# A graph kernel: TensorE reads an edge group's places four values at a time instead of up to 24

## The reference, cut to what matters

```python
edge_index = jnp.stack([src, dst])
h = jnp.maximum(_layernorm(x, axis=-1), 0.0)
W = jnp.zeros((1024, 1024)).at[row, col].add(edge_weight)   # row, col = src, dst
x = x + h @ W.T + L0_gnn_bias
h = jnp.maximum(_layernorm(x, axis=-1), 0.0)
# two layers, each: agg = segment_sum(h[src], dst); mean = agg / max(deg, 1)
#                   h = h @ W_self + mean @ W_neigh + b     (relu after the first)
return x + h
```

## Time and profile before

| | |
|---|---|
| median of 3 runs | 784.9 us (784.1 to 787.94) |
| the profiled execution | 788.07 us |
| its span, from the first to the last instruction | 786.3 us |
| PE busy | 748.0 us, 95% of the span |
| mean granted clock of TensorE | 0.987 of full |

### The profile page before, as it was taken

How to read it: one execution, slowest core, us unless ns; L and a number is a source line. 1 busy time by engine, 2 the same in 40 slices (tenths; PEclk the granted TensorE clock), 3 DMA queues, 4 the chain that set the end, 5 groups by cost and what they waited for, 6 DMA issues and landing times.

```text
span 786.3 us, 13475 instructions
## 1 busy us (share of the span) xinstructions
PE 748.0 (95%) x4433; PEld 619.4 (79%) x4434; DVE 584.0 (74%) x813; ACT 355.2 (45%) x596; POOL 478.5 (61%) x593
## 2 busy tenths in 40 slices
PE   2878999999999999899999999999999999999997
PEld 2767888888878788788888888888888888887886
DVE  7989378778545789985768775445698867589895
ACT  7757734333254357542325655543232223244731
POOL 5000057676748899775666382416799766755982
PEclk9689999999999999999999999999999999999999
DMA  3112455865566863465875625865843577776475
GB/s 113 43 53 90 139 156 191 257 204 187 185 214 202 280 220 97 149 212 182 301 234 178 190 91 149 291 207 200 293 162 108 194 235 261 257 249 209 155 238 193
DMA packets 82873, 148.78 MB, mean 189 GB/s; under 512 B 10795, under 2 KB 20898, under 8 KB 82800
## 3 DMA queue, kind: packets, MB, share of 16 engines
q1 hardware_dynamic: 62862, 105.07, 41.4%
q10 hardware_dynamic: 19938, 42.79, 15.3%
HBM read 106.42 MB, written 41.41 MB: 188 GB/s over the span
## 4 chain that ended last, share of the span: by engine, by line
PE 71%; DVE 13%; POOL 7%; issue 5%; DMA 2%; ACT 1%; SPq 0%; POOLq 0%; DVEq 0%; ACTq 0%
PE bank L1705 33%; PE bank L1755 20%; PE bank L1639 12%; DVE L L1938 3%; POOL split L1096 2%; DVE slot L2075 2%; DVE R L1923 2%; DVE L L1930 1%; DMA stage<-hT_scratch 1%; POOL T L1111 1%; POOL T L1113 1%; POOL S L1082 1%; PE bank L1535 1%; PE bank L1551 1%; PE bank L1771 1%
## 5 line engine op out<-in xcount | busy, mean ns | idle before, releaser
L1705 PE MATMUL bank<-slot,split 128*128 128x512 f32 x1680 | 386.4, 390 | 5.3 <-POOL split L1096 3.0
L1705 PEld LDWEIGHTS bank<-slot,split 128*128 128x128 f32 x1680 | 313.6, 188 | 72.1 <-issue 4.9
L1058 POOL TENSOR_TENSOR AT<-AT,az 128x50 int32 (+3 forms) x288 | 97.9, 340 | 120.8 <-DMA az<-asum_scratch 79.2
L1755 PE MATMUL bank<-slot,Ax 128*128 128x512 f32 x500 | 119.0, 392 | 0.2
L1096 POOL TENSOR_TENSOR split<-stage,split 128x512 fp32r<-128x512 f32 x50 | 67.3, 1348 | 76.8 <-ACT split L1324 76.7
L1755 PEld LDWEIGHTS bank<-slot,Ax 128*128 128x128 f32 x500 | 92.8, 188 | 20.3 <-issue 1.4
L2075 DVE TENSOR_TENSOR slot<-T,slot 128x512 fp32r<-128x512 f32 x64 | 91.8, 1466 | 9.7 <-ACT slot L1315 8.9
L1639 PE MATMUL bank<-slot,split_m 128*128 128x512 f32 x320 | 91.1, 396 | 0.0
L1324 ACT CAST split<-stage 128x512 fp32r<-128x512 f32 x50 | 31.1, 623 | 122.1 <-PE bank L1705 69.0
L1113 POOL TENSOR_TENSOR T<-T,wst 128x512 f32<-128x512 f32 x48 | 69.5, 1467 | 4.4 <-DMA wst<-in_L_gnn_W_self 4.4
L1639 PEld LDWEIGHTS bank<-slot,split_m 128*128 128x128 f32 x320 | 58.5, 188 | 11.1
(11 more groups left out here) (223 smaller groups left out, 1133.1 us busy)
## 6 DMA issues: line engine op xcount, KB each, us to landing
stage<-hT_scratch SPq DMA_DIRECT2D x90, 256.0 KB, 3.4
wst<-in_L_gnn_W_neigh SPq DMA_DIRECT2D x56, 256.0 KB, 4.6
wst<-in_L_gnn_W_self SPq DMA_DIRECT2D x56, 256.0 KB, 3.3
x1b_scratch<-x ACTq DMA_DIRECT2D x10, 512.0 KB, 5.3
hT_scratch<-hTs ACTq DMA_DIRECT2D x10, 512.0 KB, 3.3
wst<-prod0g_scratch SPq DMA_DIRECT2D x20, 256.0 KB, 3.5
hT_scratch<-h1s ACTq DMA_DIRECT2D x20, 256.0 KB, 3.4
wst<-prod1g_scratch SPq DMA_DIRECT2D x20, 256.0 KB, 3.7
```

The lines of the kernel that those rows point to most:

```text
L1058: pool.tensor_tensor(a, a, az32[:, n % NZ, pairs * pos:pairs * (pos + 1)], ALU.add) \
L1705: last = pe.matmul(dense_bank(v, which)[:, :], split[:, v % 2, a, NT * k:NT * (k + 1)], slot[t % 2][:, b, HF * (HK * which + k):HF * (HK * ...
L1755: last = pe.matmul(sums, Ax[:, u % NR_A, NT * k:NT * (k + 1)], part, start=(begins and k == 0 and b == 0), stop=(k == PAIRS - 1 and b == 1 ...
```

## The change

Places are no longer loaded ahead of three groups at once. Before each of the groups 3 to 36 there is a load of that group's own places: 4 values in groups 3 to 5, and from group 6 on the first four (chunks 0 to 3). The second four (chunks 4 to 7) are loaded in the middle of the group's products, before those of chunk 3. Bases are loaded only where they are used: one value ahead of group 3 (that of group 7), four in the middle of group 8 (of 10, 12, 14 and 16, every second entry of the table), then four at a time in the middle of groups 16, 20, 24, 28 and 32, before the products of chunk 4. TensorE has 68 loads of `tab_o` where it had 14, and 7 of `tab_w` where it had 4. No product, wait, DMA or instruction of another engine is added or removed.

```diff
-AT_ONCE = 24
-BASES = {3: range(4, 8), 8: range(8, 16), 15: range(16, 32), 31: range(32, LATE)}
+BASES = {3: range(7, 8), 8: range(10, 17, 2)}
+BASES.update((j, range(j + 1, j + 5)) for j in range(16, LATE - 1, 4))
@@
             def column_sums(j):
                 q, r = j % NQ, j % NR
                 for c in range(GC):
+                    if c == GC // 2 - 1 and SHARED[j] == 1:
+                        load_offsets(j, GC // 2, GC)
+                    if c == GC // 2 and j > 3 and j in BASES:
+                        load_bases(j)
@@
-            def load_offsets(j):
-
-                each = GC // SHARED[j]
-                upto = j + 1
-                while upto < LATE and SHARED[upto] == SHARED[j] and each * (upto + 1 - j) <= AT_ONCE:
-                    upto += 1
-                values = load(pe, tab_o[0:1, GC * j:GC * upto:SHARED[j]], 0, (WW - WD) * TW)
+            def load_offsets(j, first, last):
+
+                share = SHARED[j]
+                values = load(pe, tab_o[0:1, GC * j + first:GC * j + last:share], 0, (WW - WD) * TW)
+                offsets_of.update(((j, first // share + n), value) for n, value in enumerate(values))
+
+            def load_bases(j):
+
+                at = BASES[j]
+                base_of.update(zip(at, load(pe, tab_w[0:1, at.start:at.stop:at.step], 0, F)))
@@
-                if j not in offsets_of:
-                    load_offsets(j)
-                if j in BASES:
-                    if j == 3:
-                        pe.wait_ge(s_tabw, 16)
-                    base_of.update(zip(BASES[j], load(pe, tab_w[0:1, BASES[j].start:BASES[j].stop], 0, F)))
-                offsets = offsets_of[j]
+                load_offsets(j, 0, GC if SHARED[j] > 1 else GC // 2)
+                if j == 3:
+                    pe.wait_ge(s_tabw, 16)
+                    load_bases(j)
```

More of the change, by code:

```diff
@@ L1534, in column_sums @@
                     for part in range(3):
-                        last = pe.matmul(w_bank(j)[:, bass.ds(offsets[c // SHARED[j]], kw(j))], row,
+                        last = pe.matmul(w_bank(j)[:, bass.ds(offsets_of[(j, c // SHARED[j])], kw(j))], row,
                                          L[:, q, c, ka(j) + kw(j) * part:ka(j) + kw(j) * (part + 1)],
@@ L1567, in _ @@
             offsets_of, base_of = {}, {}
-            def load_offsets(j):
-                each = GC // SHARED[j]
-                upto = j + 1
-                while upto < LATE and SHARED[upto] == SHARED[j] and each * (upto + 1 - j) <= AT_ONCE:
-                    upto += 1
-                values = load(pe, tab_o[0:1, GC * j:GC * upto:SHARED[j]], 0, (WW - WD) * TW)
-                offsets_of.update((n, values[each * (n - j):each * (n - j + 1)]) for n in range(j, upto))
+            def load_offsets(j, first, last):
[5 more added lines that the diff above has]
+                base_of.update(zip(at, load(pe, tab_w[0:1, at.start:at.stop:at.step], 0, F)))
             for j in range(LATE):
```

## The result

The changed kernel took **790.69 us** (median of 4 runs, 789.9 to 791.57), the kernel before 784.55 in the same session (4 runs, 784.1 to 787.94). The ratio is **1.0059, 95% interval 1.0035 to 1.0082**: slower, by 4.6 us by the ratio and by 6.1 between the two medians. I had forecast 785.7, a range of 776 to 796, and "within 0.5%" as the likeliest. The profiled execution of the changed kernel had 791.57 us, span 789.8, mean granted clock 0.995.

What follows compares the result with a forecast made beforehand. TensorE was taken as the bound, its sequencer pacing the edge stage. Stretches of -1.1, +1.5, -1.7, +1.0, +0.8 and +0.3 summed to +0.8 us, taking the median from 784.9 to 785.7; range 776 to 796.

Steps and rivals of the forecast that it cites:

- the sequencer sets the pace: Edge stage: TensorE's sequencer, not the array (1.49 and 1.73 us a group), paces every group at 2.0 to 2.2; 62%.
- The pitch of groups without a base load: TensorE, edge stage: 1.27 + 0.39 + 0.47 = 2.13 us a group with a set end, 2.02 without.
- A hole of 0.3 before chunk 3: Sign in each group's products: about 0.3 us idle at the middle load, where the kernel before had none.
- Fours of places: TensorE's register loads of four neighbouring places: 0.37 us each, bounds 0.348 and 0.43.
- Rival B: Middle loads covered by queued products, so the array's 1.49 and 1.73 us pace groups: 773, half covered 779; 20%.
- rival C: A load amid running products costs 0.59 us, as loads of five or eight did: 14.7 us more, 800; 12%.
- rival D: Evenly spread holes keep the granted clock at half in groups 21 to 36: +13 us, 799; 6%.
- The length of a load by its fours: Register loads: values come in pieces of four, 0.10 us + 0.251 a piece; entries not neighbours one by one, 0.23 each.
- 12 to 20: Edge stage stretch: seven groups with set ends, two without, bases in 16 and 20: 19.9 against 21.62 us, -1.7.
- 27 to 35: Edge stage stretch: nine groups at 2.13 us and two base loads at 0.47: 20.1 against 19.29 us, +0.8.
- part two: Bases: five loads of four neighbours mid-group at 0.47 us each, one of every second entry in group 8 at 1.12.
- the reference: Starting point of the forecast: profiled execution of the kernel before, 788.07 us, 3.2 above the median of 784.9.

Runs made afterwards that it cites:

- experiment 4: Kernel before with at most 8 places in a load instead of 24, nothing else changed: 781.95 us, ratio 0.9939.
- 7: Kernel before with eight places read in one load ahead of each group, bases early and starting at multiples of four: 780.27 us, ratio 0.9929.
- 8: As 7, but from group 6 on places in two loads of four, the second ahead of chunk 3: 784.74 us, ratio 0.9979 to the kernel before.
- 9: As 7, but from group 6 on sixteen places (two groups) in one load: 783.2 us, ratio 0.9947 to the kernel before.
- experiment 1: Changed kernel with base ranges moved to start at multiples of four, eight middle loads where six stood: 787.88 us, ratio 1.0024 to the kernel before.
- experiment 3: Kernel before with only the bases loaded as in the changed kernel, places still 24 at once: 791.6 us, ratio 1.0081.
- 2: Kernel before with only the places loaded as in the changed kernel, bases as before: 785.63 us, ratio 1.0008.
- 5: Changed kernel with each middle load of places written twice; the pairs were merged, so the same kernel again: 790.99 us, ratio 1.0054 to the kernel before.
- 10: As 7, but bases 16 to 36 in one load in group 2, none later: 778.89 us, ratio 0.9895 to the kernel before.

## Why the prediction was right, and where it was not

The time lay inside the range, 5 us above the number; "within 0.5%", the likeliest outcome, did not come, and "slower", held at 0.30, did. The path was the one forecast, one term of its sum was too small by a factor of three, and the range was wide enough for that.

**What held.** That the sequencer sets the pace, and the model of its time. The pitch of groups without a base load, forecast at 2.13 with a set end and 2.02 without, was 2.14 in group 25; the five of groups 21 to 26 other than 24 average 2.07. A hole of 0.3 before chunk 3 was forecast, 0.29 came. Fours of places were forecast at 0.37 and took 0.33, strided ones at 1.02 and took 0.99. The same sums gave the pitch of experiment 4 (1.88, measured 1.90) and the difference of 7 and 8 (5, measured 4.61). Rival B (covered loads, 20%) fell by the changed kernel's own pitch and by 7 and 8; rival C (0.59 us for a short load amid products) by the 33 loads with a median of 0.332; rival D by the clock of 1.00 from group 21 on. The length of a load by its fours held too: 0.10 + 0.25 a piece makes 0.60 for eight neighbours and 1.10 for sixteen, and they took 0.59 (experiment 4) and 1.12 (9) in the median. That the entry at which a four begins counts as well, experiment 1 shows: 0.337 us in the median where the changed kernel's took 1.00 to 1.20.

**Stretch by stretch**, forecast against measured: to group 6 -1.1, measured -1.41; groups 6 to 11 +1.5, +1.27; 12 to 20 -1.7, -0.30; 21 to 26 +1.0, +1.18; 27 to 35 +0.8, +2.38; group 36 +0.3, +0.34. The two that miss most are those with two base loads each. Groups 21 to 26, with one, hide it, as their other loads came cheaper than 0.37.

**The step that failed** is part two, "five loads of four neighbours ... at 0.47 each". They took 1.20, 1.20, 1.00, 1.00 and 1.11 us: 5.53 where 5 x 0.37 = 1.85 was counted, 3.7 too little. Experiment 1 gives it back by moving the ranges (3.53 us at the last product, all but 0.35 of it by loads of this kind), and experiment 3 has it without the places' part. I had the piece of four from the rows of before, but every load there starts at a multiple of four, so these could not show what it hangs on; I took "neighbours" for the condition. The ranges 17 to 20, 21 to 24 stood in the diff. An operation whose start the trace never showed should have had 1.02, the price of the strided four, as its upper bound; then the case would have reached 5 x (1.02 - 0.37) = 3 us further up.

**The second miss** is the reference. The stage was late by 3.46 us, the medians differ by 6.1 and the ratio says 4.6. I carried the profiled execution's 3.2 us above the median over as a constant. It was not one: the changed kernel's profiled execution lies 0.9 above its median. Before's had a mean granted clock of 0.987, while 26 other executions of it, run beside experiments 1 to 4 on another chip, had 0.984 to 0.998, on average 0.992, and on the whole a lower clock went with a longer time (five at 0.997 and above took 782.75 to 785.03 us, five at 0.986 and below 786.97 to 790.57; but the fastest of all, 781.9, had 0.992). In the profile of before what is missing of the clock lies in the stage, in the earlier trace rows's groups 6 to 20 with their 0.61 and 0.75. So part of the gain that I summed there was probably against a stretch slower than usual. How much of the 2.7 us this makes up, and how much is chance in single executions, the runs don't separate.

With the base loads at their real price the forecast would have been 785.7 + 3.7 = 789.4, and slower the likeliest. The stage would then have stood at +0.8 + 3.7 = +4.5 against +3.46 measured, so the other terms, the fours at 0.37 among them, were 1.0 us too dear together: that the forecast was no further off is in part luck.

**Two readings that don't come out of their rows.** The load at 67.27 was covered for 0.8 us, not 0.6: the next product came 2.17 us after its start, and TensorE was idle for 1.39 of that the earlier trace rows. And rival D's price: clearing a bank took 0.63 / 0.38 = 1.66 times as long, which makes 1.49 and 1.73 into 2.5 and 2.9 and not 2.7 and 3.1, so +9 us and 795, inside the range and not beyond it. Neither bears on the result.

**Why fours were the wrong size.** From group 6 on the ten loads of 24 of before took 1.86 us on average, 0.62 a group; 1.61, or 0.54 a group, was the shortest of them. Eight took 0.60 on average in experiment 4, sixteen 1.19 in 9, and fours 0.345 in the changed kernel, 0.69 a group, or 0.79 with a restart of 0.1. So halves are the dearest for the sequencer, and the other three are nearly alike. What then sets 24 behind eight was not tried by itself. The rows fit two things: the load outlasts the products queued ahead of it by more (the hole of 0.46 a group against 0.17), and VectorE waited 3.3 us for TensorE to free its tiles, but never at eight.

## What to carry to other kernels

Read register values in whole pieces of four that begin at a multiple of four, even if some are not needed: here three unused values were nearly free (0.31 us for one, 0.33 for four), and a start one entry above such a multiple made the load three times as long (1.00 to 1.26 us). Put one short load ahead of each batch of products, and none into its middle: there the products covered almost nothing of it (a hole of 0.29 us for a load of 0.33), and where the issuing sequencer is the bound, a load cut in two only adds to its time (2 x 0.33 us against 0.59, and 4.61 us at the last product between 7 and 8). And before a cost model taken from rows is used on new operands, ask which property all those rows shared.

## What the runs showed of the hardware

- A register load of four neighbours took 0.33 us when it began at a multiple of four (places: 33 loads, 0.326 to 0.553; bases in experiment 1: 8 loads, 0.327 to 0.561) and 1.00 to 1.26 when it began one above (entries 17, 21, 25, 29 and 33; 10 loads in the changed kernel and experiment 3; other starts were not tried), as long as four that are not neighbours (0.99) or longer. Eight took 0.59 and sixteen 1.12 in the median, at most 0.83 and 1.35.
- A load in the middle of a stream of products, 0.33 us long, opens a hole of 0.29 us with 8-wide products (chunk 2 of group 24 began at 63.24, chunk 3 at 63.66): the products ahead of it covered almost none of it.
- Kernels with loads of at most 16 places were granted a higher clock on average over their runs: 0.995 to 1.000 (the changed kernel and experiments 1, 2, 4, 5 and 7 to 10), against 0.990 in experiment 3 and 0.991 to 0.993 for the kernel before in its three sessions, both with 24 places a load. Why was not tried.
